# Attention tower with a routed feed-forward part: heads multiplied on GpSimd, evictions moved to ScalarE, two gate buffers, and the last batch's quarters interleaved

## The chip, the cores and the metric

The kernel runs on one core of one Trainium2 chip. The metric is the device time of one execution in microseconds (us). The engines are TensorE (PE in the rows; its weight loads are PEld), VectorE (DVE), ScalarE (ACT), GpSimd (POOL) and SyncE (SP), which here only issues DMAs.

## The reference

```python
h = tok(x)                       # gather per token: sin/cos waves @ W_proj + biases, (8, 1024, 512)
h = h + attn(layernorm(h))       # 16 heads of 32; S = K Q^T * scale, causal, minus (i - j);
                                 # softmax over j, times V, then @ o_w.T
h = h + ffn(layernorm(h))        # scores = sqrt(softplus(h @ gate_w.T)); top 6 of 32 experts;
                                 # place of a token in an expert = count of earlier choices, at most 192;
                                 # silu(g) * u per expert; plus a shared expert: clip(silu(sg h) * (su h), 10) @ sd.T
```

All of it is float32, for 8 batches of 1024 tokens.

## The kernel before

The program has three parts, run one after the other: `embed` (the gathers, the first layernorm, which writes `d_hidden` and the transposed `d_normed_t` to HBM), `attend` (attention, router and shared expert, which scatters each token's normalised row to its six places in `d_slots`), and `experts` (the 32 routed experts, added to `out`). The change is in `attend`.

`attend` first projects q, k and v of two head groups (12 projections, the prologue), while SyncE loads constants. Then it walks over 32 steps: 8 batches of 4 head groups (g = 0 to 3, four heads each). A step has 12 slots, m = 0 to 11. Slots 0 to 3 are the score tiles of the first 512 query rows, slots 4 to 11 those of the second 512. In each slot TensorE does the scores of the slot (`scores`, L1309, with the shift L1313 and the mask L1319), the product with the values of the slot before (`attend_group`, L1332), and row scores for the next step's maxima (`row_scores`, L1285). ScalarE turns the scores into probabilities (`soften`, L872), GpSimd adds them up (`add_probs`, L806) into `first_probs`, two buffers `probs` going round, and VectorE takes row maxima (`row_maxima`, L994).

In between, at three gaps A, B and C of each slot, lie the uses of one PSUM bank, `ps_dense`, in an order fixed at build time (`plan`): the projections for a later step (`project`, L1273 and L1269), the sums of the probabilities (`sum_probs`, L1341), the turned row maxima (`turn_maxima`, L1292), the output projection of the batch before (`out_project`, L1352, only in g = 0), and one quarter (256 tokens) of the router and shared expert of the batch before: `turn` (L1360), `route` (L1367), `up` twice (L1375), `place` (`count_earlier`, L1391), `down` twice (L1383). Each use waits until the one before has been taken out of the bank (`dense_free`). In before, VectorE takes out the values (L986) and the row shifts (L1008), ScalarE the projections of q and k, the sums (L885), the turned rows and the gate inputs (L903, L904).

VectorE's division of the heads by the sums (`divide_heads`) is cut into four pieces of 128 columns for each half of a step: a reciprocal (L1015) and a multiply (L1018) each, in slots 1 to 4 (late half of the step before) and 6, 8, 9, 10 (early half). `out_project` and the next `take_sums` wait for `heads_done`, given by the fourth piece. VectorE's queue in slot 10 is: row maxima, the early half's fourth piece, `gate(x, 1)` (L1153 plus one, L1155 reciprocal, L1158 and L1160 multiplies, L1162 clamp), then `find_places`, whose first instruction (L1127) empties the bank. TensorE's next use is `down` at slot 11, gap A.

After the 32 steps the last batch still lacks its output projections and its four quarters. Before, these run one after the other: eight `out_project` with `add_residual` and a store and reload through `d_hidden`, then four times `quarter` (statistics, normalise, turn, route, up, choose, place, down), each ending in 12 scatters by GpSimd (L810). `experts` begins when all is stored.

## Time and profile before

| | |
|---|---|
| time of the kernel, median of 3 runs | 3867.13 us (3866.15 to 3868.62) |
| profiled execution: its own time, its span | 3872.97 us, 3871.2 us |
| mean granted TensorE clock | 0.920 of full |
| busy over the span: PE, DVE, ACT, POOL | 84%, 63%, 29%, 43% |
| last `embed` DMA issue, first projection of `attend` | 249.32 us, 281.15 us |
| first step begins, first tail quarter's `down` | 367 us, 766 us |
| the 32 steps end, the `experts` loads begin | about 3323 us, 3541.29 us |

Times in the profile are microseconds from the start of the span. A busy share is an average over the whole span; what a part of the change is worth has to be read from its own stretch.

### The profile page before, as it was taken

The page shows a single profiled execution, that of the slowest core. Times are in us where ns is not written, and L with a number is a line of the kernel's source. Part 1 is how long each engine was busy: PE and PEld are TensorE (multiplying, and loading weights), DVE is VectorE, ACT ScalarE, POOL GpSimd, SP SyncE. Part 2 cuts the span into 40 slices and gives each one's busy share as a digit, 9 for nine tenths or more (in the row PEclk, how much of TensorE's full clock was granted, in tenths as well). Part 3 has the DMA queues.
Part 4 walks back from the last instruction along what each step waited for, and adds up shares of the span by engine and source line. Part 5 has one row for each costly group of instructions (what it writes and reads, how often), then busy time and mean ns, then how long its engine had stood idle before and what let it go on. Part 6 is the DMA issues. An engine that isn't in the chain of part 4 may idle for free. (4 is left out here: it accounts for less than half of the span.)

```text
span 3871.2 us, 62509 instructions
## 1 busy us (share of the span) xinstructions
PE 3245.3 (84%) x20296; PEld 1670.1 (43%) x20296; DVE 2419.5 (63%) x6622; ACT 1112.7 (29%) x2553; POOL 1671.2 (43%) x924
## 2 busy tenths in 40 slices
PE   4647999888888888888888888889888977655998
PEld 2324444444444444444444444444444433334776
DVE  6733565567667665766576657665776577553554
ACT  3751333233223322332233223322332233101111
POOL 5630354445435443544454445444444446322332
PEclk8878999999999999999999999999999988867999
DMA  5664000021111011101010101010101000104996
GB/s 199 244 271 136 1 28 20 28 77 50 68 51 46 14 34 34 34 12 39 29 34 12 40 28 34 12 40 28 34 12 39 28 12 12 55 25 133 259 259 154
DMA packets 123205, 257.87 MB, mean 67 GB/s; under 512 B 38988, under 2 KB 39628, under 8 KB 120192
## 3 DMA queue, kind: packets, MB, share of 16 engines
q1 hardware_dynamic: 78400, 201.42, 15.8%
q0 software_dynamic: 44048, 49.26, 5.0%
q8 instruction: 169, 2.77, 0.3%
q10 hardware_dynamic: 432, 3.15, 0.2%
q14 instruction: 156, 1.28, 0.1%
HBM read 146.71 MB, written 204.26 MB: 91 GB/s over the span
## 5 line engine op out<-in xcount | busy, mean ns | idle before, releaser
L806 POOL TENSOR_TENSOR a_first_probs<-a_first_probs,a_probs 128x2048 f32<-128x2048 f32 (+3 forms) x320 | 1033.5, 3230 | 1594.1 <-ACT a_probs L872 1375.0
L994 DVE CUSTOM_DVE_ANT_0 a_unused<-a_ps_ring,a_decay 128x512 bf16<-128x512 f32 (+3 forms) x1536 | 773.4, 554 | 515.8 <-PE a_ps_ring L1285 510.2
L872 ACT ACTIVATE a_probs<-a_ps_ring 128x512 f32<-128x512 f32 (+3 forms) x1280 | 505.5, 473 | 794.8 <-PE a_ps_ring L1319 600.1
L810 POOL DMA_INDIRECT d_slots<-a_rows,a_place_i x397 | 395.6, 997 | 226.3 <-DVE a_place_i L1147 141.7
L1309 PE MATMUL a_ps_ring<-a_k_t,a_q_t 32*128 32x512 f32 (+3 forms) x3072 | 412.6, 539 | 72.4 <-DVE a_row_max L994 44.0
L1285 PE MATMUL a_ps_ring<-a_q_t,a_k_t 32*128 32x512 f32 (+3 forms) x3072 | 391.3, 542 | 17.5 <-DVE a_row_max L994 12.6
L1383 PE MATMUL a_ps_dense<-a_sd,a_inner_t 128*128 128x512 f32 x256 | 184.5, 860 | 191.3 <-DVE a_gate_up L1127 188.0
L1273 PE MATMUL a_ps_dense<-a_normed_t,a_q_w 128*128 128x512 f32 x512 | 246.0, 625 | 35.1 <-DVE a_max_cols L980 32.5
L872 ACT ACTIVATE a_first_probs<-a_ps_ring 128x512 f32<-128x512 f32 x256 | 135.6, 605 | 475.8 <-PE a_ps_ring L1319 450.9
L1332 PE MATMUL a_ps_heads<-a_probs,a_values 128*32 128x512 f32 (+3 forms) x2560 | 269.9, 495 | 0.0
L1309 PEld LDWEIGHTS a_ps_ring<-a_k_t,a_q_t 32*128 32x128 f32 x3072 | 146.0, 186 | 274.9 <-issue 147.0
L1352 PE MATMUL a_ps_dense<-a_o_w,a_attn_t 128*128 128x512 f32 x512 | 237.9, 608 | 18.3 <-DVE a_values L986 10.5
L1273 PE MATMUL a_ps_dense<-a_normed_t,a_k_w 128*128 128x512 f32 x512 | 238.4, 609 | 15.7 <-DVE a_residual L1025 9.7
L1269 PEld LDWEIGHTS a_ps_dense<-a_v_w,a_normed_t 128*128 128x128 f32 x2048 | 235.1, 193 | 36.5 <-issue 35.5
L1269 PE MATMUL a_ps_dense<-a_v_w,a_normed_t 128*128 128x128 f32 x2048 | 247.3, 279 | 1.7 <-ACT a_k_t L857 0.9
L1015 DVE RECIPROCAL a_sum_inv<-a_sum_inv 128x128 f32<-128x128 f32 x256 | 242.6, 948 | 1.9 <-ACT a_sum_inv L885 1.9
L1285 PEld LDWEIGHTS a_ps_ring<-a_q_t,a_k_t 32*128 32x128 f32 x3072 | 144.8, 187 | 225.2 <-issue 189.6
L1018 DVE TENSOR_TENSOR a_attn_t<-a_attn_t,a_sum_inv 128x128 f32<-128x128 f32 x256 | 221.8, 866 | 14.3 <-DVE a_sum_inv L1015 0.9
L1008 DVE CAST a_row_shift<-a_ps_dense 128x512 bf16<-128x512 f32 x64 | 44.3, 692 | 238.0 <-PE a_ps_dense L1292 238.0
L1651 POOL DMA_INDIRECT out<-x_y,x_index x64 | 90.2, 1409 | 236.1 <-DMA out<-x_y,x_index 151.9
L1383 PEld LDWEIGHTS a_ps_dense<-a_sd,a_inner_t 128*128 128x128 f32 x256 | 59.8, 259 | 272.7 <-DVE a_inner_t L1162 158.3
L1273 PEld LDWEIGHTS a_ps_dense<-a_normed_t,a_q_w 128*128 128x128 f32 x512 | 95.7, 197 | 160.2 <-issue 152.8
(177 smaller groups left out, 4402.2 us busy)
## 6 DMA issues: line engine op xcount, KB each, us to landing
d_hidden<-e_hidden SPq DMA_DIRECT2D x8, 2048.0 KB, 7.9
d_normed_t<-e_normed_t SPq DMA_DIRECT2D x8, 2048.0 KB, 11.6
a_normed_t<-d_normed_t SPq DMA_DIRECT2D x8, 2048.0 KB
a_residual<-d_hidden SPq DMA_DIRECT2D x64, 256.0 KB
d_hidden<-a_residual SPq DMA_DIRECT2D x64, 256.0 KB
a_hidden<-d_hidden SPq DMA_DIRECT2D x64, 256.0 KB
out<-a_hidden SPq DMA_DIRECT2D x64, 256.0 KB
x_w_gate<-w_gate SPq DMA_DIRECT2D x32, 512.0 KB, 6.3
```

The lines of the kernel that those rows point to most:

```text
L806: nc.gpsimd.tensor_tensor(total_of, total_of, probs_of(m)[:, :, 0:width], ALU.add).then_inc(added, 1)
L810: nc.gpsimd.indirect_dma_start(slot_rows, bass.IndirectOffsetOnAxis(ap=place_i[p][:, j, choice:choice + 1], axis=0), rows[p][:, j, :], Non ...
L872: nc.scalar.activation(probs_of(m)[:, h, 0:width], score_bank(m, h)[:, 0:width], ACT.Exp).then_inc(exp_done, 1)
L994: nc.vector.tensor_tensor_reduce(unused[:, h, 0:width], row_bank(k, h)[:, 0:width], decay[:, at:at + width], 1.0, NEG, ALU.add, ALU.max, r ...
L1015: nc.vector.reciprocal(sum_inv[half][:, cols], sum_inv[half][:, cols]).then_inc(sums_inverted, 1)
L1269: mm = nc.tensor.matmul(ps_dense[:, t * P:(t + 1) * P], normed_t[:, c, tile * P:(tile + 1) * P], w[:, c, g * P:(g + 1) * P], start=(c == 0 ...
L1273: mm = nc.tensor.matmul(ps_dense[:], w[:, c, g * P:(g + 1) * P], normed_t[:, c, half_cols(half)], start=(c == 0), stop=(c == DC - 1))
L1285: nc.tensor.matmul(row_bank(k, h)[:, 0:width], k_t[g][dims, i * P:(i + 1) * P], q_t[g][dims, j0:j0 + width], start=True, stop=True).then_i ...
L1309: nc.tensor.matmul(score_bank(m, h)[:, 0:width], q_t[st.g][dims, j * P:(j + 1) * P], k_t[st.g][dims, i0:i0 + width], start=True, stop=False)
L1332: mm = nc.tensor.matmul(ps_heads[dims, at], values[g][:, j, dims], probs_of(m)[:, h, 0:width], start=(j == 0), stop=(j == last_j))
L1352: mm = nc.tensor.matmul(ps_dense[:], attn_t[:, g, i * P:(i + 1) * P], o_w[:, g, :], start=(g == 0), stop=(g == G - 1))
L1383: mm = nc.tensor.matmul(ps_dense[:], inner_t[:, m, j * P:(j + 1) * P], sd[:, m, :], start=(m == 0), stop=(m == MC - 1))
```

## The change

- `divide_heads` is split. VectorE keeps the four reciprocals (`invert_sums`); GpSimd multiplies a whole half, 128x512, at once (`multiply_heads`), before its add of slot 5 (late half) and slot 11 (early half), and gives `heads_done`.
- ScalarE takes the values and the row shifts out of `ps_dense`.
- The gate: `exp` goes into `inner_t`, ScalarE adds the one there, and each of the two `up` halves has its own `gate_up` buffer; VectorE's gate has four instructions for five. The wait of ScalarE for `inner_done` in `soften_gate` is gone.
- Router: two small instructions are folded into others, `counts` (float32) is dropped for running counts in bf16, updated in `find_places`; `count_earlier` has four small matmuls for two.
- The scratch output `unused` has three parts instead of four. GpSimd gives `rows_free` in slot 0 instead of slot 1.
- After the 32 steps: all eight residual tiles are loaded to SBUF at once into q and k tiles that are no longer in use (not stored and reloaded), PSUM uses go round four banks of the score ring, and output projections, statistics, normalising and turning of quarter q + 1 are placed between the parts of quarter q (`late_uses`). Each quarter has its own row buffer and places.
- First loads: the first half of `normed_t` is loaded by itself, the biases of q and k go to ScalarE's queue behind `q_w`; TensorE waits for the constants only before `turn_maxima`; the 33 stores that empty the slots are issued after the prologue.

The tables of slots (`QUARTER_AT`, `STATS_AT`, ...) hold the same slots as before.

```diff
+            def multiply_heads(s, g, half):
+                heads = attn_t[:, g, half_cols(half)]
+                pool.wait_ge(heads_taken, 2 * s + half + 1)
+                pool.wait_ge(sums_inverted, PIECES * (2 * s + half + 1))
+                nc.gpsimd.tensor_tensor(heads, heads, sum_inv[half][:], ALU.mult).then_inc(heads_done, 1)
...
             def step(st):                                    # GpSimd
                 for m in range(N_GROUPS):
+                    if m == LATE_MULTIPLY and not st.first:
+                        multiply_heads(st.s - 1, (st.g - 1) % G, 1)
+                    if m == EARLY_MULTIPLY:
+                        multiply_heads(st.s, st.g, 0)
                     add_probs(st, m)
...
+            def take_values(g, half, use):                   # ScalarE; VectorE's is gone
+                act.wait_ge(use.full, use.n + 1)
+                nc.scalar.activation(values[g][:, half_tiles(half), :], use.bank[:].rearrange("p (t m) -> p t m", m=P),
+                                     ACT.Identity).then_inc(use.free, 1)
...
+            def take_maxima(p, half, use):                   # ScalarE; VectorE's is gone
+                act.wait_ge(use.full, use.n + 1)
+                nc.scalar.activation(row_shift[p][:, half_cols(half)], use.bank[:], ACT.Identity).then_inc(use.free, 1)
...
-                if m > 0:
-                    act.wait_ge(inner_done, MC * x + m)
-                act.wait_ge(dense_full, n + 1)
-                nc.scalar.activation(gate_e[:], ps_dense[:, 0:2 * P], ACT.Exp, scale=-1.0).then_inc(gate_e_done, 1)
-                nc.scalar.activation(gate_up[:], ps_dense[:], ACT.Identity).then_inc(dense_free, 1)
+                act.wait_ge(use.full, use.n + 1)
+                nc.scalar.activation(inner_t[:, m, :], use.bank[:, 0:2 * P], ACT.Exp, scale=-1.0).then_inc(gate_e_made, 1)
+                nc.scalar.activation(gate_up[m][:], use.bank[:], ACT.Identity).then_inc(use.free, 1)
+                act.wait_ge(gate_e_made, MC * x + m + 1)
+                nc.scalar.activation(inner_t[:, m, :], inner_t[:, m, :], ACT.Identity, bias=1.0).then_inc(gate_e_done, 1)
...
-            def divide_heads(s, g, half, piece, n):          # VectorE
+            def invert_sums(half, piece, use):
+                cols = slice(piece * HALF // PIECES, (piece + 1) * HALF // PIECES)
+                dve.wait_ge(use.free, use.n + 1)
                 nc.vector.reciprocal(sum_inv[half][:, cols], sum_inv[half][:, cols]).then_inc(sums_inverted, 1)
-                dve.wait_ge(heads_taken, 2 * s + half + 1)
-                dve.wait_ge(sums_inverted, PIECES * (2 * s + half) + piece + 1)
-                instruction = nc.vector.tensor_tensor(heads, heads, sum_inv[half][:, cols], ALU.mult)
...
                 if st.g == G - 1:                            # SyncE
-                    for i in range(2):
-                        load_residual(st.b, i)
+                    if st.rows:
+                        for i in range(2):
+                            load_residual(st.b, i)
+                    else:
+                        sp.wait_ge(scores_full, ITEMS * (FINAL - 2))
+                        for i in range(NT):
+                            sp.dma_start(late_hidden[i], dram["hidden"][NB - 1, tile_rows(i), :]).then_inc(late_in, 16)
...
+    uses = out(0, 0) + out(0, 1) + [("sums", 1, None)] + turn(0, 0) + turn(0, 1)
+    for q in range(QUARTERS):
+        uses += [("route", 0, q), ("up", 0, q)] + out(q + 1, 0) + [("up", 1, q)] + out(q + 1, 1) + [("place", 0, q)]
+        uses += turn(q + 1, 0) + turn(q + 1, 1) + [("down", 0, q), ("down", 1, q)]
...
+            def quarter(q):                                  # VectorE, last batch
+                soft_parts(late("route", 0, q), chain)
+                soft_sum(x, chain)
+                gate(x, 0, late("up", 0, q), chain)
+                if more:
+                    add_late(2 * q + 2, late("out", 2 * q + 2))
+                choose(x, chain)
+                if more:
+                    add_late(2 * q + 3, late("out", 2 * q + 3))
+                    take_late_stats(q + 1, norm)
+                count_chosen(chain)
+                if more:
+                    normalise_late(q + 1, norm)
+                gate(x, 1, late("up", 1, q), chain)
+                find_places(x, q, late("place", 0, q), chain)
+                for j in range(2):
+                    add_shared(late_hidden[2 * q + j], late("down", j, q))
...
-            pe.wait_ge(consts_in, 16 * N_CONSTS)             # TensorE
-            pe.wait_ge(consts_made, N_MADE)
...
-            pe.wait_ge(normed_in, 16)
+            pe.wait_ge(normed_half_in, 16)
             for n, (kind, half) in enumerate(PROJECTIONS * 2):
+                if n == 2:
+                    pe.wait_ge(normed_in, 16)
...
+            sp.wait_ge(dense_full, N_PROLOGUE)               # SyncE, before the 33 stores
```

## Rows read from the trace of the kernel before

**Rows 1.** Busy time by stretch (last steps and after): us, each engine, granted clock, DMA share, GB/s

```profile
770.00:3130.00 2360.00, 2099.12 (x14101) 1013.78 (x14094) 1579.80 (x4558) 705.27 (x1686) 1092.57 (x543) 0.95 0.11 34
3130.00:3325.00 195.00, 141.42 (x986) 64.91 (x986) 145.93 (x340) 56.73 (x144) 105.57 (x55) 0.82 0.05 14
3325.00:3545.00 220.00, 116.20 (x328) 69.46 (x328) 91.61 (x276) 18.81 (x50) 56.93 (x58) 0.73 0.14 42
```

**Rows 2.** Waits of TensorE, 770 to 3130: total us, times, longest

```profile
PE a_ps_dense L1383 <- DVE a_gate_up L1127: 153.9, 24, 6.7
PE a_ps_dense L1375 <- DVE a_values L986: 29.0, 19, 1.5
PE a_ps_ring L1309 <- DVE a_row_max L994: 17.7, 37, 0.8
...
PE a_ps_dense L1352 <- DVE a_values L986: 9.0, 6, 1.6
```

**Rows 3.** Timeline, 1026 to 1032, one quarter's end: start, us, instruction

```profile
1026.09 1.49 DVE L1018 TENSOR_TENSOR a_attn_t<-a_attn_t,a_sum_inv 128x128 f32<-128x128 f32 x1
1026.13 1.29 POOL L806 TENSOR_TENSOR a_first_probs<-a_first_probs,a_probs 128x512 f32<-128x512 f32 x1
...
1027.51 0.28 DVE L1153 TENSOR_SCALAR a_gate_e<-a_gate_e 128x256 f32<-128x256 f32 x1
...
1030.83 0.55 DVE L1127 TENSOR_TENSOR a_gate_up<-a_is_top,a_ps_dense 128x384 f32<-128x384 bf16 x1
...
1031.51 3.78 PE L1383 MATMUL a_ps_dense<-a_sd,a_inner_t 128*128 128x512 f32 x4 [6.34 <-DVE a_gate_up L1127]
```

**Rows 4.** The multiplies L1018, 770 to 3130: shortest/median/longest ns

```profile
L1018 DVE TENSOR_TENSOR a_attn_t<-a_attn_t,a_sum_inv x197: 291/805/2187, 787.0 to 3117.7; 128x128 f32<-128x128 f32 x197
```

**Rows 5.** Busy time by stretch, two microseconds inside that `down`

```profile
1034.00:1036.00 2.00, 2.00 (x10) 0.20 (x8) 0.68 (x1) 0.00 (x0) 0.00 (x0) 0.50 0.00 0
```

**Rows 6.** Groups of GpSimd by form, 900 to 3100

```profile
L806 POOL TENSOR_TENSOR a_first_probs<-a_first_probs,a_probs 128x512 f32<-128x512 f32 x46 | 58.6, 1274 | 81.7 <-ACT a_probs L872 81.5
```

**Rows 7.** Groups of VectorE by form, 900 to 3100: count | busy, mean ns | idle before

```profile
L986 DVE COPY a_values<-a_ps_dense 128x512 f32<-128x512 f32 x46 | 31.5, 686 | 0.8 <-issue 0.8
```

**Rows 8.** Groups of ScalarE by form, 900 to 3100

```profile
L904 ACT ACTIVATE a_gate_up<-a_ps_dense 128x512 f32<-128x512 f32 x46 | 27.2, 592 | 0.0
```

**Rows 9.** Waits of TensorE, 3130 to 3325, the last batch's steps

```profile
PE a_ps_dense L1383 <- DVE a_gate_up L1127: 14.4, 3, 6.2
PE a_ps_ring L1309 <- ACT a_probs L872: 14.0, 6, 5.7
PE a_ps_ring L1309 <- DVE a_row_max L994: 10.9, 8, 5.1
PE a_ps_dense L1391 <- DVE a_counts L1116: 7.8, 2, 4.6
```

**Rows 10.** Timeline after the 32 steps, 3325 to 3542

```profile
3325.55 3.70 PE L1352 MATMUL a_ps_dense<-a_o_w,a_attn_t 128*128 128x512 f32 x8 [0.78 <-ACT a_sum_inv L885]
...
3372.95 0.23 DVE L1058 TENSOR_SCALAR a_plus<-a_ps_dense 128x64 f32<-128x64 f32 x1 [6.92 <-PE a_ps_dense L1367]
...
3394.87 0.98 POOL L810 DMA_INDIRECT d_slots<-a_rows,a_place_i  x1 [57.34 <-DVE a_place_i L1147]
...
3535.26 0.98 POOL L810 DMA_INDIRECT d_slots<-a_rows,a_place_i  x1 [0.30 <-issue]
...
3541.29 0.34 SPq L1505 DMA_DIRECT2D x_ident<-c_ident  x1
```

**Rows 11.** Timeline of the first loads and the first projection

```profile
259.79 0.43 ACTq L845 DMA_DIRECT2D a_q_w<-q_w  x1
...
281.15 5.87 PE L1273 MATMUL a_ps_dense<-a_normed_t,a_q_w 128*128 128x512 f32 x8 [32.48 <-DVE a_max_cols L980]
```

**Rows 12.** DMA issues, 225 to 345: KB each, median us to landing

```profile
a_q_w<-q_w ACTq DMA_DIRECT2D x1, 1024.0 KB, 9.5
```

**Rows 13.** Timeline of the first batch, a projection behind slot 11's row maxima

```profile
444.31 6.22 PE L1273 MATMUL a_ps_dense<-a_normed_t,a_q_w 128*128 128x512 f32 x8
```

More of the change, by code:

```diff
@@ L450 @@
 N_PROBS = 2
+N_UNUSED = HG - 1
 ADDS = N_GROUPS - 2
@@ L453 @@
 SOFT_LEAST = 2.0 ** -62
-PIECES = HALF // P
 QUARTERS = 4
@@ L651, in attend, with late, dense @@
         N_CONSTS = len(consts) + 3
-        N_MADE = 3
+        N_MADE = 2
         FREE = 16
         SCATTERS = 16 * 2 * TOPK
-        TAIL_STEPS = 49
+        NORM_STEPS, TAIL_STEPS = 8, 35
+        @dataclass
+        class Use:
+            bank: object
+            full: object
+            free: object
+            n: object
+        def late(kind, arg, q=None):
+            n = next(n for n, (k, a, u) in enumerate(LATE) if (k, a) == (kind, arg) and (q is None or u == q))
+            k = n % LATE_BANKS
+            return Use(ps_ring[k], late_full[k], late_free[k], n // LATE_BANKS)
+        def dense(n):
+            return Use(ps_dense, dense_full, dense_free, n)
         def shape(m):
@@ L1028, in take_stats, with take_late_stats @@
+            def take_late_stats(q, norm):
+                for j in range(2):
+                    use = late("out", 2 * q + j)
+                    dve.wait_ge(use.free, use.n + 1)
+                take_stats(late_hidden[2 * q:2 * q + 2], norm)
+            def take_stats(tiles, chain):
                 dve.wait_ge(tail_consts_in, 16 * len(tail_consts))
                 for j in range(2):
-                    dve.wait_ge(hidden_in[j], 16 * (x + 1))
-                    chain.done(nc.vector.bn_stats(stats[:, j, :], hidden[j][:]))
+                    chain.done(nc.vector.bn_stats(stats[:, j, :], tiles[j]))
@@ L1177, in take_dense, with add_shared @@
+            def add_shared(tile, use):
+                dve.wait_ge(use.full, use.n + 1)
+                nc.vector.tensor_tensor(tile, use.bank[:], tile, ALU.add).then_inc(use.free, 1)
+            def take_dense(st, slot, gap, chain):
+                for kind, arg, k in st.uses[slot][gap]:
+                    use = dense(st.base + k)
+                    if kind == "out":
+                        add_residual(st.t, arg, use)
                     elif kind == "route":
-                        soft_parts(n, chains[0])
+                        soft_parts(use, chain)
@@ new lines, in tail_events @@
+            def tail_events(st, m, after, norm, chain):
+                x, first = QUARTERS * st.t + st.g, st.g == 0
+                if (m, after) == STATS_AT[first]:
+                    for j in range(2):
+                        dve.wait_ge(hidden_in[j], 16 * (x + 1))
+                    take_stats([tile[:] for tile in hidden], norm)
+                if (m, after) == NORMALISE_AT[first]:
+                    dve.wait_ge(rows_free, x + 1)
+                    normalise(x, rows[st.g % 2], [tile[:] for tile in hidden], norm)
+                if (m, after) == SOFT_SUM_AT[first]:
@@ L1252, in _ @@
+            norm = norm_chain(0)
+            take_late_stats(0, norm)
+            for piece in range(PIECES):
+                invert_sums(1, piece, late("sums", 1))
+            normalise_late(0, norm)
             for q in range(QUARTERS):
```

536 lines of the change are left out of this document (272 added, 264 removed).

## The prediction, made before the changed kernel was run

> **What bounds the kernel now.** I read the busy time by stretch first [rows 1]. Over 770 to 3130 (24 steps with a tail quarter) TensorE is busy 2099 of 2360 us, 89%; nothing else is above 67%. So TensorE sets the pace, and a change can win only the 261 us in which it stands still there, and time lost to its clock. In the last batch's steps TensorE is busy 73%, VectorE 75%; after the steps, 53% at a granted clock of 0.73.
>
> Next, the waits of TensorE in the first of these stretches [rows 2]. One wait is more than half of all idle time: `down` behind L1127, 153.9 us in 24 times, 6.4 us each, once per quarter. Then 38.0 us behind VectorE's eviction of values (L1375 and L1352), and 17.7 us behind row maxima.
>
> The timeline says what makes that one wait [rows 3]. `down` waits for the bank, the bank for L1127, and L1127 for its place in VectorE's queue: the last piece of the division, then the gate. The multiply L1018 of 128 columns takes 1.49 us there, and ends 0.16 us after GpSimd's add L806, which runs at the same time. Over the steady part L1018 takes 805 ns at the median against 291 ns at its shortest [rows 4]: it stretches when a GpSimd add runs. After the stall the granted clock is 0.50, that is 1.2 GHz instead of 2.4 [rows 5], and the four matmuls of `down` take 3.78 us, about twice what the second `down` of the same quarter takes.
>
> **The change part by part.**
>
> *The division.* VectorE loses 8 multiplies per step, 8 x 0.8 = 6.4 us of its queue [rows 4]. GpSimd gains two 128x512 operations, 2 x 1.27 = 2.5 us [rows 6]. In the slot-10 queue the multiply's 1.49 us goes, and L1153's 0.28 us with it [rows 3], since ScalarE adds the one in good time. The row maxima of slot 10 start earlier too: values are not evicted before them (0.69 us [rows 7]). Together 1.49 + 0.28 + 0.7 = 2.5 us less per quarter. Against it stands one new collision. GpSimd's multiply waits for the fourth reciprocal, so it runs right beside the gate's reciprocal, and its add of slot 11 follows at once, with no DMA issue between. The gate's two multiplies read two SBUF tiles, as L1018 does, and would wait for whichever runs. Bounds: 0.1 us (VectorE gets in as the multiply ends) to 1.3 us (it sits through the add as well). I take 0.6 us, nearer to the first, because L1018 in [rows 3] starts within 0.2 us of the add's end. So 1.9 us per quarter (1.2 to 2.4) over the 25 such quarters before 3130: 47 us (30 to 60).
>
> The rule for this in the Trainium skill, "SBUF — State Buffer", section "Who interferes with whom", is that a VectorE instruction with two SBUF inputs and a GpSimd one that reads SBUF exclude each other for the whole instruction. The trace agrees: L1018 takes 1.49 us there against 0.29. By the rule applied without mercy the gate would sit through multiply and add, and the gain per quarter would be 1.2 us. "GPSIMD Engine Reference", section "4.1 Engine selection", speaks against the move itself: elementwise work belongs on VectorE, GpSimd is about twice as slow with two inputs. This trace doesn't bear that out at this size: 1.27 us on GpSimd against 4 x 0.29 = 1.16 on VectorE undisturbed.
>
> *Evictions on ScalarE.* The values: ScalarE has nothing before it in its queue but exps long due, so the 38.0 us of [rows 2] go; all of them, because TensorE has scores to do between that projection and its next use of the bank. The row shifts cut the other way. In slots 1 and 5 ScalarE still has two exps to do when the turned maxima are ready, where VectorE had been waiting for them; a copy of 592 ns [rows 8] after them ends some 0.15 us later than the row scores that hide it. Twice in 32 steps: 0.3 x 32 = 10 us lost (0 to 20).
>
> *Gate buffers, router.* The second buffer removes a ScalarE wait that ends before `up` is ready anyhow: 0. Fewer small VectorE instructions shorten slots 8 and 9, where TensorE doesn't wait in the steady part: 0, covered by the v projection in slot 9. The two added matmuls of `place`: about 0.2 us x 28 = 6 us lost. `unused` in three parts: the first maximum is long done when the fourth starts, 0. `rows_free` earlier: GpSimd is idle there, 0.
>
> *Row maxima.* VectorE catches up sooner; of the 17.7 us I take 8. In the first batch one wait of this kind per step is followed by a stretch at 0.50 clock in which a projection takes 6.22 us [rows 13] instead of 3.70; I take 5 us of waits and 7 of clock (half of 4 steps x 3.4).
>
> *GpSimd late half.* Its multiply in slot 5 comes before an add of 4.5 us. Before that add GpSimd is idle some 11 us in the timeline, but the fourth reciprocal comes only about 2 us before the add starts; 1.27 us fits. Behind it in the queue stand this add and the scatters; who waits for the add is ScalarE, two slots on. 0, and if the reciprocal came 1 us later, 0.3 us of it would be seen. `heads_done` comes 1 to 2 us later, ten microseconds ahead of `out_project`.
>
> *Last batch's steps.* 54 us of waits; the four of [rows 9] make 47. From `down` 3 x 1.9 = 6, from `place` (late VectorE) 5, from row maxima 5, from exps (ScalarE behind a VectorE that GpSimd holds up) 4: 20 us (8 to 32; GpSimd is the tightest in the last step, where slots take 6 us and an add with a scatter 5.9).
>
> *After the steps.* Before: 3325.5 to 3541.3, 215.8 us [rows 10]: eight projections, then four quarters, the later ones (3535.3 - 11 x 1.28 - 3394.9)/3 = 42 us apart. New: two projections end at about 3331; but `add_late` waits for all eight loads, which SyncE issues behind the last `store_out`, from about 3324 on, with 2 MB to bring: 3335.5. Statistics 1.7, four reciprocals 3.8 (they stand between statistics and normalising), normalise 1.7, turns 3.5, route 3.6: `soft_parts` at 3351 instead of 3373. A quarter then cannot be shorter than TensorE's work, 116.2/4 = 29 us [rows 1], nor longer than before with its projections, 50.6. Following the queues (up 3.9, projection 3.7, up, projection, statistics and normalise, gate, `down` twice, route of the next, partly at the lower clock) I get 33 us. Three of them, then the last quarter's 21.9 us from L1058 to the first scatter, 12 scatters in 15.4 us, and 6.0 us from the last one to `experts` [rows 10]: 3351 + 99 + 22 + 15 + 6 = 3493, 48 us saved (21 to 60, the ends being 42 us and 29 us a quarter).
>
> *First loads.* TensorE starts when `q_w` and half of `normed_t` are in. `q_w` is issued at 259.79 and lands 9.5 us later, at 269.3 [rows 11, 12], against a start at 281.15 behind the constants. k and v weights land at 272.5 and 275, before they are used; the constants still come before the first maxima. 11 us (7 to 12). The stores into the slots run later under the first steps; who needs them is GpSimd's scatter in the second batch, 350 us on: 0.
>
> The sum against the profiled execution, 3872.97: 47 + 38 + 8 + 12 + 20 + 48 + 11 = 184 won, 16 lost, 168 in all: 3705. The median of the runs lies 5.8 us below the profiled one: 3699. Of the steady stall's clock loss (5.3 us at half speed after each stall, 2.65 us x 28 = 74 us) I count only a tenth, since shorter waits than 4.4 us are followed by the lower clock in this trace too: 7. **3692 us.**
>
> **The rivals.**
>
> *The collision takes the place of the multiply* (0.2). The gate is held through GpSimd's multiply and add, and each of its later instructions meets the next GpSimd one. For it: L1018 itself, stretched from 0.29 to 0.8 at the median. Against: L1158 and L1160 never stretched before in the steady part. Then nothing of the 47 + 6 us is left: 3745.
>
> *The clock holds* (0.15). With 4.4 us for 6.4 TensorE comes back while still at 2.4 GHz, or soon returns to it. For: the step is very regular, so what happens once happens 24 times. Against: in the first batch 2.4 us of waits are enough for the lower clock. Then most of the 74 us comes on top: 3692 - 60 = 3632.
>
> *The late pipeline doesn't pipeline* (0.07). All eight loads and VectorE's single queue hold each quarter at the old 42 us: 21 us saved instead of 48: 3719.
>
> *GpSimd becomes the bound; slower than before* (0.04). Its multiply in slot 5 waits at the head of its queue for VectorE's fourth reciprocal; the 4.5 us adds slip, `probs` buffers come free late, exps and scores with them. It decides from 5.3 us per step on (168/32), against the 2 us of slack and GpSimd's 46% share [rows 1]. At 6 us per step: 3889.
>
> **How the numbers follow.** The forecast has 0.54, its own range 3655 to 3725: the ends of its terms, not all at once. With the collision and the late pipeline above it and most of the clock case below, the range for 8 in 10 is 3625 to 3750. A measurement of this kernel tells about 0.2%, 8 us, from no change. Faster 0.95, within 0.01, slower 0.04.
>
> **What would show it.** Right: the wait of `down` behind L1127 near 4.4 us, none behind values, L1153 and L1018 gone, first projection at 270, the `experts` loads some 170 us after the last `attend_group` instead of 218. Wrong: `down` still at 6 us with L1158 stretched beyond 0.43 us; waits behind ScalarE's evictions of row shifts above 0.3 us; a mean granted clock clearly above 0.95 between the steps; GpSimd's slot-5 multiply starting after the exps of slot 5.

## The result, and the profile after

The changed kernel takes **3718.6 us** (median of 4 runs, 3716.9 to 3725.4) against 3867.9 us of the kernel before on the same chip (4 runs, 3866.2 to 3872.9): ratio 0.9615, 95% interval 0.9599 to 0.9632. 149 us are gone; 3692 us were forecast, in a range of 3625 to 3750. The profiled execution took 3716.85 us (span 3715.1, granted clock 0.935 instead of 0.920), against 3872.97: 156.1 us less.

Where they went is read from five marks in both timelines: the start of the first `down` (L1383 before, L1472 after), of the `down` 24 quarters later (the last batch's first), of the last one in the steps, the first load of `experts`, and the end of the span.

| stretch, us | before | after | gained |
|---|---|---|---|
| start to the first `down` | 765.9 | 742.7 | 23.2 |
| 24 quarters | 2297.0 (95.7 each) | 2230.3 (92.9 each) | 66.6 |
| last batch's steps, first to last `down` | 253.5 | 242.9 | 10.7 |
| last `down` to `experts`' first load | 224.9 | 169.9 | 55.0 |
| `experts` | 329.9 | 329.3 | 0.6 |

Busy time by stretch, after (us, then PE, PEld, DVE, ACT, POOL, granted clock, DMA share, GB/s), the three stretches that answer to [rows 1]:

```profile
745.00:3040.00 2295.00, 2096.25 (x14159) 1018.90 (x14158) 1387.64 (x4123) 773.35 (x1834) 1157.51 (x592) 0.96 0.11 35
3040.00:3222.00 182.00, 136.02 (x967) 62.36 (x966) 134.03 (x294) 59.81 (x151) 112.07 (x59) 0.82 0.05 14
3222.00:3390.00 168.00, 101.24 (x356) 63.44 (x355) 84.78 (x251) 21.95 (x59) 58.54 (x59) 0.76 0.11 32
```

The first of them and that of [rows 1] hold nearly as many quarters each, 24.7. TensorE is as busy as before; its idle time fell from 261 to 199 us. TensorE's waits in the same stretch (total us, times, longest), which answer to [rows 2]:

```profile
PE a_ps_dense L1472 <- DVE a_gate_up L1203: 128.3, 24, 5.4
PE a_ps_ring L1398 <- DVE a_row_max L1084: 24.6, 37, 0.7
PE a_ps_dense L1449 <- ACT a_rows_t L976: 19.2, 25, 0.8
```

No wait behind values is left. The wait of `down` fell from 6.4 to 5.35 us, not to 4.4. The timeline of one quarter's end shows why; beside [rows 3], L1018 and L1153 are gone, and L1234 (L1158 before) has become long:

```profile
995.02 0.95 DVE L1099 RECIPROCAL a_sum_inv<-a_sum_inv 128x128 f32<-128x128 f32 x1
...
995.88 1.70 DVE L1231 RECIPROCAL a_inner_t<-a_inner_t 128x256 f32<-128x256 f32 x1
996.05 1.28 POOL L862 TENSOR_TENSOR a_attn_t<-a_attn_t,a_sum_inv 128x512 f32<-128x512 f32 x1
997.27 1.27 POOL L855 TENSOR_TENSOR a_first_probs<-a_first_probs,a_probs 128x512 f32<-128x512 f32 x1
997.70 1.13 DVE L1234 TENSOR_TENSOR a_inner_t<-a_gate_up,a_inner_t 128x256 f32<-128x256 f32 x1
...
999.33 0.49 DVE L1238 TENSOR_SCALAR a_inner_t<-a_inner_t 128x256 f32<-128x256 f32 x1
999.75 0.54 DVE L1203 TENSOR_TENSOR a_gate_up<-a_is_top,a_ps_dense 128x384 f32<-128x384 bf16 x1
...
1000.41 3.40 PE L1472 MATMUL a_ps_dense<-a_sd,a_inner_t 128*128 128x512 f32 x4 [5.35 <-DVE a_gate_up L1203]
```

The gate's first multiply, 0.43 us when nothing is in its way, starts at 997.70 inside GpSimd's addition (997.27 to 998.54) and ends at 998.83, just behind it. That is 0.70 us of the 1.73 us that L1018 and L1153 gave back (before, from L1018's start at 1026.09 to L1155's at 1027.82). The clamp L1238 takes 0.49 us instead of 0.29; beside it GpSimd issues a scatter (998.71 to 999.72).

The first projection and the stretch behind the steps, in the timeline, which answer to [rows 10, 11]:

```profile
271.81 5.90 PE L1362 MATMUL a_ps_dense<-a_normed_t,a_q_w 128*128 128x512 f32 x8 [22.21 <-DMA a_normed_t<-d_normed_t]
...
3223.55 7.13 PE L1441 MATMUL a_ps_ring<-a_o_w,a_attn_t 128*128 128x512 f32 x16
...
3248.01 0.23 DVE L1146 TENSOR_SCALAR a_plus<-a_ps_ring 128x64 f32<-128x64 f32 x1 [5.93 <-PE a_ps_ring L1456]
...
3276.89 1.00 POOL L866 DMA_INDIRECT d_slots<-a_rows,a_place_i  x1 [36.07 <-DVE a_place_i L1225]
...
3365.56 0.98 POOL L866 DMA_INDIRECT d_slots<-a_normed_t,a_place_i  x1 [9.40 <-DVE a_place_i L1225]
...
3385.77 0.34 SPq L1604 DMA_DIRECT2D x_ident<-c_ident  x1
```

From the first out projection to `soft_parts` 24.5 us instead of 47.4, and from the first quarter's first scatter to the last quarter's (88.7 us apart) 29.6 us per quarter instead of 42.

### The profile page after: what moved, and what is told of

It is laid out like the page before. It is cut to its first block and busy times, and to the rows that moved or that the text cites. A ratio compares the mean times of both kernels' runs of the same rounds, so it can differ in the third digit from the quotient of the medians.

```text
span 3715.1 us, 61950 instructions
## 1 busy us (share of the span) xinstructions
PE 3207.5 (86%) x20352; PEld 1660.1 (45%) x20360; DVE 2157.7 (58%) x6046; ACT 1201.6 (32%) x2745; POOL 1756.5 (47%) x988
## 3 DMA queue, kind: packets, MB, share of 16 engines
q14 instruction: 148, 1.21, 0.1%
## 5 line engine op out<-in xcount | busy, mean ns | idle before, releaser
L1398 PE MATMUL a_ps_ring<-a_k_t,a_q_t 32*128 32x512 f32 (+3 forms) x3072 | 412.0, 538 | 66.6 <-DVE a_row_max L1084 44.4
L866 POOL DMA_INDIRECT d_slots<-a_rows,a_place_i x373 | 379.2, 1017 | 134.4 <-issue 71.6
L1472 PE MATMUL a_ps_dense<-a_sd,a_inner_t 128*128 128x512 f32 x224 | 158.8, 848 | 147.4 <-DVE a_gate_up L1203 147.4
L1362 PE MATMUL a_ps_dense<-a_normed_t,a_q_w 128*128 128x512 f32 x512 | 240.5, 613 | 24.7 <-DMA a_normed_t<-d_normed_t 22.2
L862 POOL TENSOR_TENSOR a_attn_t<-a_attn_t,a_sum_inv 128x512 f32<-128x512 f32 x64 | 81.6, 1274 | 280.3 <-DVE a_sum_inv L1099 279.7
L1441 PE MATMUL a_ps_dense<-a_o_w,a_attn_t 128*128 128x512 f32 x448 | 206.2, 603 | 1.1 <-ACT a_row_shift L965 0.2
L1362 PEld LDWEIGHTS a_ps_dense<-a_normed_t,a_k_w 128*128 128x128 f32 x512 | 92.3, 190 | 143.4 <-issue 112.4
L1402 PE MATMUL a_ps_ring<-a_row_shift,a_key_shift 5*128 5x512 bf16 (+3 forms) x1536 | 154.7, 328 | 0.0
```

Of the source, the lines that this page charges most:

```text
L866: nc.gpsimd.indirect_dma_start(slot_rows, bass.IndirectOffsetOnAxis(ap=place_i[p][:, j, choice:choice + 1], axis=0), late_rows[p][:, j, :] ...
L1362: mm = nc.tensor.matmul(use.bank[:], w[:, c, g * P:(g + 1) * P], normed_t[:, c, half_cols(half)], start=(c == 0), stop=(c == DC - 1))
L1398: nc.tensor.matmul(score_bank(m, h)[:, 0:width], q_t[st.g][dims, j * P:(j + 1) * P], k_t[st.g][dims, i0:i0 + width], start=True, stop=False)
L1441: mm = nc.tensor.matmul(use.bank[:], attn_t[:, g, i * P:(i + 1) * P], o_w[:, g, :], start=(g == 0), stop=(g == G - 1))
```

## The experiments

All start from the changed kernel. Each was timed in 5 rounds beside the kernel before, whose median was 3869 to 3872 us; 8 us decide. One more thing varies between the profiles in the first stretch: up to the first `down`, `late_serial` has the instructions of the changed kernel, yet it gets there at 749.8 us instead of 742.7, with a granted clock of 0.97 instead of 1.00 from 380 to 500 us (the kernel before has 0.97 there). Some 7 us of a profile can be this; what decides between the two is not shown.

### The division back on VectorE: `divide_back`

```diff
-                nc.gpsimd.tensor_tensor(heads, heads, sum_inv[half][:], ALU.mult).then_inc(heads_done, 1)
...
+                dve.wait_ge(sums_inverted, PIECES * (2 * s + half) + piece + 1)
+                instruction = nc.vector.tensor_tensor(heads, heads, sum_inv[half][:, cols], ALU.mult)
```

> The changed kernel (3718.6 us) with the division wholly on VectorE again, four multiplies of 128x128 a half, and no multiply on GpSimd. Theory 1 (the multiply on GpSimd shortens VectorE's chain ahead of the down matmuls, but only by what is left after a collision): the stall ahead of L1472 goes from 5.35 us to 6.1 to 6.5, about as before the change, and the kernel loses 28 quarters by 0.8 to 1.1 us, 22 to 31 us, plus up to 12 us for the four late pieces: 3740 to 3762. Rival (the multiply gained nothing there; the 1.0 us that the stall lost came from the one that adds 1 and from the clock): 3718 within 8 us, stall 5.2 to 5.6.

Measured: 3754.6 us (ratio 0.9698, 0.9683 to 0.9714), 36 us slower. Theory 1 holds. The waits of `down`:

```profile
PE a_ps_dense L1466 <- DVE a_gate_up L1197: 154.4, 25, 6.3
```

This is nearly as much as before the change, 6.2 us each for 6.4. In the 24 quarters the division is worth 25 us (2255.4 against 2230.3), a little over 1 us each.

### Is the gate held by GpSimd? `invert_slot7` and `multiply_slot10`

```diff
-LATE_INVERT, EARLY_INVERT = (1, 2, 3, 4), (6, 8, 9, 10)
+LATE_INVERT, EARLY_INVERT = (1, 2, 3, 4), (6, 7, 8, 9)
...
-LATE_MULTIPLY, EARLY_MULTIPLY = 5, 11
+LATE_MULTIPLY, EARLY_MULTIPLY = 5, 10
```

The first has the first pair of lines alone, the second both.

> The early reciprocals stand in slots 6, 7, 8, 9 instead of 6, 8, 9, 10, so the 0.95 us reciprocal of slot 10 leaves the chain row maxima, reciprocal, gate, down. GpSimd's multiply stays in slot 11, before its addition. Theory 1 (the gate's first multiply is held until GpSimd's addition of slot 11 ends, at 998.54 us in the profiled quarter): the reciprocal of the gate ends 0.95 us sooner, its multiply starts 0.95 us sooner and is held 0.95 us longer, about 2.1 us in all instead of 1.13; the stall stays at 5.2 to 5.4 us and the time within 8 us of 3718.6. Rival (VectorE's own instructions alone set the stall): stall 4.4 us, 28 quarters by 0.95 us = 27 us faster, 3692.

Measured: 3716.6 us (0.9606, 0.9587 to 0.9626), stall 5.3 us in every quarter (128.1 us, 24 times). Taking 0.95 us out of VectorE's queue ahead of the gate gains nothing: the rival falls. The timeline of the same place shows where it went. The gate's first multiply now takes 1.93 us:

```profile
995.59 1.93 DVE L1234 TENSOR_TENSOR a_inner_t<-a_gate_up,a_inner_t 128x256 f32<-128x256 f32 x1
995.95 1.28 POOL L855 TENSOR_TENSOR a_first_probs<-a_first_probs,a_probs 128x512 f32<-128x512 f32 x1
```

In all 24 quarters of 745 to 3040 it takes 1.93 to 2.04 us, where the changed kernel has 1.13 to 1.27. GpSimd, not VectorE's own work, set the gate's end.

> The same early reciprocals in slots 6 to 9, and GpSimd's early multiply in slot 10 ahead of that slot's addition instead of in slot 11. Theory 1 (collision): GpSimd's addition of slot 11 now runs about 1.2 us sooner, the gate's multiply waits 0.5 us at most, and the stall falls to 3.8 to 4.2 us: 28 quarters by 1.2 to 1.5 us, 33 to 42 us faster than the changed kernel, 3677 to 3686, of which the multiply now in slot 9 to 10 may give back up to 8 us by holding the count of chosen experts. Rival (no collision): the same as with the reciprocals moved alone, 3692.

Measured: 3724.8 us (0.9619, 0.9604 to 0.9634), no gain. The stall did fall, to 4.1 us at most (94.9 us in 24 times), as Theory 1 had it, but both theories had the time wrong. What was gained came back elsewhere. TensorE's waits, and the place in the timeline where they come from:

```profile
PE a_ps_dense L1472 <- DVE a_gate_up L1203: 94.9, 24, 4.1
PE a_ps_dense L1480 <- DVE a_chosen_b L1196: 40.1, 18, 2.8
```

```profile
991.64 3.66 DVE L1196 CAST a_chosen_b<-a_soft_ln 128x64 bf16<-128x64 f32 x1
991.64 1.31 POOL L862 TENSOR_TENSOR a_attn_t<-a_attn_t,a_sum_inv 128x512 f32<-128x512 f32 x1
...
992.87 2.36 POOL L855 TENSOR_TENSOR a_first_probs<-a_first_probs,a_probs 128x1024 f32<-128x1024 f32 x1
```

A cast of 128x64 that takes 0.20 us in the changed kernel takes 3.66, through GpSimd's multiply and the addition behind it. I had foreseen this at 8 us at most; it cost 40 us of waits. The multiply had been moved from one thing that matters to another.

### The second gate earlier: `gate_slot9` and `gate9_invert7`

```diff
-GATE_AT = {True: ((7, 1), (10, 1)), False: ((7, 1), (10, 1))}
+GATE_AT = {True: ((7, 1), (9, 1)), False: ((7, 1), (9, 1))}
```

The second has the early reciprocals in slots 6 to 9 as well.

> The second gate (reciprocal 1.70 us, two multiplies, clamp) is computed at the end of slot 9, after the count, instead of at the end of slot 10. VectorE stands idle for 1.5 us there in the profiled quarter, so the row maxima of slot 10 start about 2.2 us later than now and end about 2.2 us later, and behind them only the reciprocal 0.95 and the multiply L1203 0.54 stand before the bank is free. Theory 1: down starts 1.0 to 1.5 us sooner, 28 to 42 us faster: 3677 to 3691, while TensorE's wait for the row maxima at slot 11's scores grows by up to 2.2 us and the stall at the down matmuls shrinks to about 2 us. Rival (the later row maxima cost as much as the gate gains): 3718 within 8 us.

Measured: 3697.5 us (0.9548, 0.9533 to 0.9563), 21 us faster, short of the 28 to 42. The stall is nearly gone, but it has moved:

```profile
PE a_ps_ring L1398 <- DVE a_row_max L1084: 97.3, 38, 3.8
PE a_ps_dense L1472 <- DVE a_gate_up L1203: 24.2, 24, 1.4
```

121.5 us of waits instead of 152.9. In its timeline the gate's first multiply takes 1.77 us through the addition of slot 10, which my 1.0 to 1.5 us for the whole part had not allowed for.

> The second gate in slot 9 (alone: 3697.5 us, 21 us faster than the changed kernel) and the early reciprocals in slots 6 to 9 (alone: 3716.6, no change). Theory 1 (VectorE's queue from the count to L1203 bounds slot 10; the reciprocal moved out was worth nothing only because GpSimd's addition held the gate, and with the gate gone ahead nothing holds it): the 0.95 us reciprocal leaves the path, down starts up to 0.9 us sooner: 15 to 25 us faster than 3697.5, 3672 to 3683. Rival (the parts add up): 3695.5 within 8 us.

Measured: 3705.9 us (0.9571, 0.9556 to 0.9585): not faster than `gate_slot9`, 8 us slower, at the edge of what can be told. Neither theory had it. The `down` wait is gone (1.3 us in all), and the row maxima's has grown to 117.0 us: with the reciprocals done early GpSimd multiplies at once, and now the clamp is held, an instruction with a single input:

```profile
991.11 1.83 DVE L1238 TENSOR_SCALAR a_inner_t<-a_inner_t 128x256 f32<-128x256 f32 x1
991.50 1.29 POOL L862 TENSOR_TENSOR a_attn_t<-a_attn_t,a_sum_inv 128x512 f32<-128x512 f32 x1
```

### The evictions: `values_back`, `divide_values_back`, `maxima_back`

```diff
-                nc.scalar.activation(values[g][:, half_tiles(half), :], use.bank[:].rearrange("p (t m) -> p t m", m=P),
-                                     ACT.Identity).then_inc(use.free, 1)
+                nc.vector.tensor_copy(values[g][:, half_tiles(half), :],
+                                      use.bank[:].rearrange("p (t m) -> p t m", m=P)).then_inc(use.free, 1)
```

> The changed kernel (3718.6 us) with the values evicted by VectorE again (0.69 us each, 64 of them), everything else as changed. Theory 1 (on VectorE these evictions stand behind the row maxima and hold the single dense bank): the waits behind the values come back, 38 us of them before the change; 3745 to 3757. Rival (those waits had only stood where another wait for VectorE would have stood, so moving them gained a part): 3728 to 3740.

Measured: 3722.6 us (0.9618, 0.9601 to 0.9635), 4 us and no difference that counts. Both theories fall: the waits behind values come back as 5.7 us in 6 times, not 38.

> The changed kernel with both the division and the evictions of values on VectorE again; each alone measured 36 us and 4 us slower than the changed kernel's 3718.6. Theory 1 (the 38 us of waits behind the values came from VectorE running late behind the division, so that either edit alone removes them): they come back only now: 3754.6 + 25 to 38 = 3780 to 3793, with 20 to 38 us of TensorE's waits behind values. Rival (the two parts add up): 3754.6 + 4 = 3759, within 8 us.

Measured: 3758.6 us (0.9713, 0.9700 to 0.9727). The parts add up; the waits behind values are 5.7 us again. So neither the eviction nor the division had made the 38 us. The timelines of slot 7 show what is left; first the kernel before:

```profile
1001.36 4.53 POOL L806 TENSOR_TENSOR a_first_probs<-a_first_probs,a_probs 128x2048 f32<-128x2048 f32 x1 [1.54 <-ACT a_probs L872]
...
1003.80 2.24 DVE L1153 TENSOR_SCALAR a_gate_e<-a_gate_e 128x256 f32<-128x256 f32 x1
...
1009.08 0.68 DVE L986 COPY a_values<-a_ps_dense 128x512 f32<-128x512 f32 x1
...
1009.82 1.99 PE L1375 MATMUL a_ps_dense<-a_rows_t,a_sg 128*128 128x256 f32 x8 [1.54 <-DVE a_values L986]
```

and `divide_values_back`:

```profile
982.38 4.53 POOL L855 TENSOR_TENSOR a_first_probs<-a_first_probs,a_probs 128x2048 f32<-128x2048 f32 x1 [1.54 <-ACT a_probs L929]
...
984.82 1.75 DVE L1221 RECIPROCAL a_inner_t<-a_inner_t 128x256 f32<-128x256 f32 x1
986.69 0.50 DVE L1224 TENSOR_TENSOR a_inner_t<-a_gate_up,a_inner_t 128x256 f32<-128x256 f32 x1
...
988.10 0.67 DVE L1058 COPY a_values<-a_ps_dense 128x512 f32<-128x512 f32 x1
...
989.23 1.99 PE L1459 MATMUL a_ps_dense<-a_rows_t,a_sg 128*128 128x256 f32 x8
```

In slot 7 of the kernel before, the instruction that adds 1, 0.29 us by itself, started inside GpSimd's 4.53 us addition and took 2.24 us. The gate behind it, the eviction behind the gate and TensorE's wait of 1.54 us all follow. With the addition of 1 on ScalarE the gate begins with a reciprocal, which takes its usual 1.75 us beside GpSimd, and its multiply comes as GpSimd ends and takes 0.50 us. Counted from the start of GpSimd's addition, the eviction comes at 5.72 us instead of 7.72.

The whole steady part of the kernel before agrees. From 770 to 3130 TensorE waits behind the values 19 times at L1375, and each of these waits ends 6.0 us after the start of an L1153 that took 2.23 to 2.25 us; in the quarters of g = 0, where L1153 of slot 7 took 0.29 us, L1375 has no such wait. The list of groups, 900 to 3100, had a sign of it, a mean of 1006 ns for an instruction of 0.28:

```profile
L1153 DVE TENSOR_SCALAR a_gate_e<-a_gate_e 128x256 f32<-128x256 f32 x46 | 46.3, 1006 | 0.0
```

The additions of 1 were not put back alone, so this cause is read from timelines and not tested. The six waits at L1352, 9.0 us, are another case: they are there in `values_back` too, with 5.7 us, and these the eviction on ScalarE does remove.

The row shifts go back by the same edit in `take_maxima`.

> The changed kernel with the row shifts evicted by VectorE again (64 evictions, 0.3 to 0.7 us each). Theory 1 (this part neither gained nor lost, since the evictions of row shifts were waited for on neither engine): 3718.6 within 8 us. Rival A (on ScalarE they stand behind exps, so taking them back gains up to 10 us): 3708 to 3713. Rival B (VectorE's time in slots 1 and 5 was short, so taking them back loses 28 x 2 x 0.3 us): 3735.

Measured: 3726.7 us (0.9626, 0.9608 to 0.9644), 8 us slower, at the edge of what can be told. Of the three cases Rival A falls: the move to ScalarE cost nothing. Between Theory 1 and Rival B this does not decide.

### The last batch one quarter after the other: `late_serial`

```diff
-        uses += [("route", 0, q), ("up", 0, q)] + out(q + 1, 0) + [("up", 1, q)] + out(q + 1, 1) + [("place", 0, q)]
-        uses += turn(q + 1, 0) + turn(q + 1, 1) + [("down", 0, q), ("down", 1, q)]
+        uses += [("route", 0, q), ("up", 0, q), ("up", 1, q), ("place", 0, q), ("down", 0, q), ("down", 1, q)]
+        uses += out(q + 1, 0) + out(q + 1, 1) + turn(q + 1, 0) + turn(q + 1, 1)
```

VectorE's `quarter` is ordered to match.

> The changed kernel with the last batch's quarters one after the other: both out projections, statistics, normalisation and turn of quarter q+1 follow the down projection of quarter q on TensorE and VectorE; four banks, early loads and late tiles stay. Theory 1 (the pipeline hides most of the next quarter's front): three fronts of add 1.4, statistics 1.4, rstd 2, normalisation 1.5, turn and eviction 2.5 and route, about 10 to 14 us each, come back on the path: 30 to 42 us slower, 3749 to 3761. Rival (what shortened the stretch was loading the residuals early and no longer storing and loading each tile, not the order): 3722 to 3733.

Measured: 3749.1 us (0.9685, 0.9666 to 0.9704), 30 us slower, Theory 1. The last `down` of the steps starts at 3223.21, the first load of `experts` at 3419.16: 196.0 us, between the 169.9 of the changed kernel and the 224.9 of before. The order is worth 26 us of the 55; the other 29 are left for the early loads, the four banks and the stores left out, none of which was put back alone.

### TensorE waits for the constants again: `first_wait_back`

```diff
+            pe.wait_ge(consts_made, N_MADE)
             pe.wait_ge(normed_half_in, 16)
```

> The changed kernel with TensorE waiting for the constants (all five loads and the copies made of them) before its first projection, as before the change; the loads' new order stays. Theory 1 (that wait alone held the first projection at 281 us instead of 272): first projection at 279 to 282 us, 7 to 10 us slower, 3726 to 3729. Rival (the row maxima of the first step need the same constants, so that the projections' head start is lost at once): 3718.6 within 3 us.

Measured: 3734.5 us (0.9647, 0.9631 to 0.9663), 16 us slower. The first projection starts at 281.92:

```profile
281.92 5.71 PE L1362 MATMUL a_ps_dense<-a_normed_t,a_q_w 128*128 128x512 f32 x8 [32.85 <-DVE a_max_cols L1074]
```

That is 10.1 us later, and the same 8.6 us remain at the first scores. The rival falls. The rest up to 16 us stays open; in this profile the granted clock from 380 to 500 us is 0.97, as in `late_serial`.

### Versions that keep the gate out of GpSimd's way: `split_gate` and `gate_first`

```diff
                     count_chosen(chain)
+                    invert_gate(x, 1, chain)
                 if (m, after) == GATE_AT[first][1]:
-                    gate(x, 1, dense(st.number("up", 1)), chain)
+                    gate(x, 1, dense(st.number("up", 1)), chain, inverted=True)
```

`invert_gate` is the gate's reciprocal; the reciprocals of the sums stand in slots 6 to 9.

> Early reciprocals in slots 6 to 9, and of the second gate only the reciprocal (1.70 us) in slot 9, in the 1.5 us in which VectorE stood idle; its two multiplies and the clamp stay in slot 10 behind the row maxima, where GpSimd's addition of slot 10 is over and that of slot 11 hasn't begun. Theory 1 (VectorE's queue and the collisions set the stall): behind the row maxima of slot 10 only 0.43 + 0.43 + 0.49 + 0.54 = 1.9 us stand before the bank is free instead of 5.2, so the stall of down falls from 5.35 us to 1.8 to 2.6 us and the wait behind the row maxima stays under 1 us: 28 quarters by 2.7 to 3.5 us = 76 to 98 us, less some collision: 3625 to 3650. Rival (the gate's first multiply meets GpSimd's multiply of slot 11 and its addition and is held for 1 to 2.5 us): stall 3 to 4.5 us, 3665 to 3690. Neither counts a gain of clock; if the shorter stall also spares TensorE its lower clock, up to 2 us a quarter come on top.

Measured: 3703.8 us (0.9568, 0.9552 to 0.9584), 15 us faster: outside both ranges, but with the rival's mechanism, at a higher price than its 1 to 2.5 us:

```profile
1001.10 3.31 DVE L1241 TENSOR_TENSOR a_inner_t<-a_gate_up,a_inner_t 128x256 f32<-128x256 f32 x1
1001.61 1.29 POOL L862 TENSOR_TENSOR a_attn_t<-a_attn_t,a_sum_inv 128x512 f32<-128x512 f32 x1
1002.83 1.29 POOL L855 TENSOR_TENSOR a_first_probs<-a_first_probs,a_probs 128x512 f32<-128x512 f32 x1
```

One multiply of 0.43 us takes 3.31, through two instructions of GpSimd, and the stall is 4.67. `gate_first` takes away what holds it, and puts `attend_group` ahead of `down`:

```diff
-QUARTER_AT = {True: ((4, A), (4, B), (5, C), (6, C), (8, C), (10, C), (11, A), (11, C)),
+QUARTER_AT = {True: ((4, A), (4, B), (5, C), (6, C), (8, C), (10, C), (11, B), (11, C)),
...
+                    if m == N_GROUPS - 1 and st.t is not None:
+                        pool.wait_ge(inner_done, MC * (QUARTERS * st.t + st.g + 1))
                     add_probs(st, m)
...
+                    if m == EARLY_MULTIPLY:
+                        multiply_heads(st.s, st.g, 0)
```

The last two lines stand behind the slot's scatter.

> A version meant to keep the gate out of GpSimd's way: as split_gate (early reciprocals in slots 6 to 9, the second gate's reciprocal in slot 9, its rest in slot 10), and GpSimd waits for the gate before its addition of slot 11, and multiplies only behind that addition and the slot's scatter; the first down stands behind attend_group of slot 10. Theory 1 (in split_gate the gate's second multiply was held 3.31 us through GpSimd's multiply and addition, and this alone kept its stall at 4.67 us): the second multiply takes at most 0.9 us (it may still end with the scatter of slot 10), down's wait is 1.5 to 2.4 us, 0.6 us of it because attend_group now stands ahead of it; 28 quarters by 2.9 to 3.8 us = 81 to 106 us faster than the changed kernel in waits, 3612 to 3638, if nothing waits for the later addition. Rival (the later addition and multiply hold the count, the places or the exps instead): 3650 to 3690, with new waits behind L1480, L1398 or the exps of more than 30 us.

Measured: **3628.7 us** (5 runs, 3624.7 to 3633.1; ratio 0.9371, 0.9350 to 0.9391), 90 us faster than the changed kernel and 241 us faster than the one before. Theory 1 holds. TensorE's waits over 745 to 3040, and one quarter's end:

```profile
PE a_ps_dense L1482 <- DVE a_gate_up L1207: 30.3, 25, 1.2
PE a_ps_ring L1408 <- DVE a_row_max L1088: 28.4, 42, 1.3
PE a_ps_dense L1482 <- DVE a_hidden L1251: 22.7, 24, 2.1
```

```profile
985.42 0.42 DVE L1245 TENSOR_TENSOR a_inner_t<-a_gate_up,a_inner_t 128x256 f32<-128x256 f32 x1
985.88 0.29 DVE L1247 TENSOR_SCALAR a_inner_t<-a_inner_t 128x256 f32<-128x256 f32 x1
...
986.42 1.26 POOL L855 TENSOR_TENSOR a_first_probs<-a_first_probs,a_probs 128x512 f32<-128x512 f32 x1 [0.49 <-DVE a_inner_t L1247]
...
986.77 3.48 PE L1482 MATMUL a_ps_dense<-a_sd,a_inner_t 128*128 128x512 f32 x4 [1.21 <-DVE a_gate_up L1207]
...
988.83 1.30 POOL L862 TENSOR_TENSOR a_attn_t<-a_attn_t,a_sum_inv 128x512 f32<-128x512 f32 x1
```

128 us of waits have become 53 (30.3 and 22.7; the second `down` now waits for the addition to `hidden`, which stands behind the places). The 24 quarters take 2154.8 us instead of 2230.3, 89.8 each. Beside `split_gate` this version changes two things at once, GpSimd's order and `attend_group` ahead of `down`. The gate's multiplies of 0.45 and 0.42 us show what the first does; `attend_group` fills 0.64 us of the former stall at the place shown. What each is worth in time was not measured.

## Why the prediction was right, and where it was not

The bound was named rightly: TensorE's idle time, most of it at `down`. The sum was 27 us too good, and two of its terms, the values and the first batch, were near in size without their reasons having been right or shown.

- **The down stall.** The term of 1.9 us a quarter was mis-sized: 1.0 us, 26 us over 24 quarters instead of 46. The 1.49 and 0.28 us went as worked out, and the collision was 0.7 us against the 0.6 taken. That this was so near is partly luck: the reason given for 0.6 was misread, since in [rows 3] L1018 starts at 1026.09, beside the add's start, and it is its end that comes within 0.2 us of the add's. The step that failed is "the row maxima of slot 10 start earlier too", 0.7 us: they wait for the row scores (VectorE stands idle 1.50 us ahead of them, at 993.09), so the eviction ahead of them had cost nothing. The kernel before shows the same: its row scores end at 1023.03 and its row maxima start at 1023.20, 0.17 us later with the eviction just ahead of them, and in the changed kernel it is 0.17 us as well (992.92 and 993.09). The rest is the clamp's 0.2. `divide_back` puts the whole part at 36 us. The rival in which the collision takes everything falls with it, but `invert_slot7` shows that the collision had become the bound: a further 0.95 us saved ahead of the gate was lost in it. The sentence beside the term, by the Trainium skill's "SBUF — State Buffer", section "Who interferes with whom", came to 1.2 us a quarter and so nearer to the measured 1.0 than my 1.9.
- **GpSimd's speed.** The prediction has one 128x512 multiply on GpSimd, 1.27 us, level with four of 128x128 on VectorE, 1.16 us. That sets one instruction against four. The same trace has VectorE's multiply of the same size, two inputs in SBUF, at 0.68 us (L266, in `embed`): GpSimd is 1.9 times as slow, and so the trace does bear out the factor of two that the prediction set aside.
- **The values.** The 38 us of waits went, as forecast, and the step that explains them failed. "ScalarE has nothing before it in its queue but exps long due, so the 38.0 us of [rows 2] go" took the waiting instruction's releaser for the cause. `values_back` and `divide_values_back` leave 5.7 us of these waits with VectorE evicting. By the timelines the cause of the 29.0 us at L1375 was L1153 in slot 7, held 2.24 us, for which the prediction had no term: it priced L1153 in slot 10 alone, at 0.28. [Rows 2] named who released; the timeline of that slot, or L1153's mean of 1006 ns, would have named who was late.
- **Row maxima.** Wrong in sign, by a little: 24.6 us instead of 17.7, where 8 less were taken; and the waits behind `rows_t` (L1449) are now 19.2 us.
- **Row shifts on ScalarE.** The loss of 10 us isn't there: the waits for them are 0.4 us over 745 to 3040, and `maxima_back` is not faster. The lower bound, 0, was right.
- **The clock.** Busy time fell by 0.25 us a quarter, 6 us over 24, against 7 taken. The case in which the clock holds did not come: `down` runs at 3.4 to 3.8 us behind each stall of 5.3.
- **The first loads and the first batch.** 11 + 12 us against 23.2 measured, 9.3 up to the first projection and 13.9 behind it. That the sum fits so well is luck: some 7 us of a profile can lie in the clock of this stretch, and waits and clock of the first batch were not taken apart. The wait for the constants is the whole of the earlier start, as `first_wait_back` shows.
- **The last batch's steps.** 20 us were taken (8 to 32), some 9 measured: 7.8 from the second `down` to the fourth, and 1.5 from there to the first out projection. The term for `place` failed: TensorE waits 9.5 us there once, and 13.2 in all, where [rows 9] had 7.8. In the timeline VectorE comes late because GpSimd's additions hold it: in the last step four of its instructions, each at most 0.3 us at its shortest, take 4.92, 5.04, 4.67 and 3.25 us beside them (L1155, L1160, L1238, L1172). The kernel before has three above 3 us, 4.82, 4.80 and 4.49 us (L1018, L1072, L1162). One of the four, and the wait:

```profile
3187.77 5.04 DVE L1160 TENSOR_TENSOR a_soft<-a_soft,a_soft_w 128x64 f32<-128x64 f32 x1
3188.15 4.56 POOL L855 TENSOR_TENSOR a_first_probs<-a_first_probs,a_probs 128x2048 f32<-128x2048 f32 x1
...
3210.52 0.21 PE L1480 MATMUL a_ps_dense<-a_chosen_b,a_before_b 128*128 128x64 bf16 x1 [9.55 <-DVE a_chosen_b L1196]
```

- **After the steps.** 216 us down to 168 were forecast, by the first out projection and `experts`' first load; 162.2 measured (3385.8 - 3223.6). To `soft_parts` 24.5 us against 25.5 forecast; a quarter 29.6 against 33. `late_serial` shows the order to be worth 26 us.
- **GpSimd as the bound, slower** did not come: of TensorE's waits over 745 to 3040 only 7.3 us are behind exps, 4.4 and 2.9, none of them above 0.5 us. The time given for this case was wrong by its own terms: 6 us in each of 32 steps on top of 3692 is 3884, not 3889.

The parts put back one by one come to 36 + 4 + 8 + 30 + 16 = 94 us of the 149; the 4 and the 8 can't be told from nothing. What is left lies with what was never put back alone: the addition of 1 and its buffers (by the timelines most of the 2297.0 - 2252.2 = 44.8 us by which the 24 quarters of `divide_values_back` are shorter than those of the kernel before), and the loads and banks of the last batch (29 us). Why `first_wait_back` loses 16 us and not 10 stays open.

## What to carry to other kernels

A wait's releaser is the last instruction of a queue, not its cause: go back along that queue until one instruction takes longer than it does elsewhere. A group whose mean is far above its shortest instruction is the place to start. Where VectorE and GpSimd share a stretch, when their instructions run is worth more than how many they are: moving 1.5 us of work from VectorE to GpSimd gained 1.0 us a quarter, and reordering, with no work removed, so that the gate's arithmetic meets none of GpSimd's, gained another 3.1 (92.9 to 89.8, with `attend_group` ahead of `down` included). Before an instruction is moved out of the way of one, look at what it then stands beside.

## What the runs showed of the hardware

GpSimd's arithmetic held VectorE in more than instructions with two SBUF inputs: a cast of 128x64 took 3.66 us instead of 0.20, a clamp with one input 1.83 instead of 0.29, the addition of 1 2.24 instead of 0.29. Reciprocals (1.70 to 1.75 us for 128x256) and the row maxima (0.55 us for 128x384), which read PSUM and SBUF, kept their time beside the same GpSimd instructions. The Trainium skill, "SBUF — State Buffer", section "Who interferes with whom", lists copies, casts and `tensor_scalar` among those that can take the shared pair of ports when their operands meet its conditions; these rows agree.

Nor did VectorE get in between two GpSimd instructions that follow each other at once: the 3.66 and 3.31 us last through multiply and addition both. Beside a scatter the gate's second multiply ran undisturbed (0.43 us at 998.87 in the changed kernel, scatter from 998.71 to 999.72), while the clamp behind it took 0.49 us instead of 0.29.

The clock fell behind each wait of 5.3 us that I looked at, and not behind each of 1.2: in `gate_first` the first `down`, after 1.23 us, ran in 1.98 us at a granted clock of 1.00 (2.4 GHz), the one at 986.77, after 1.21 us, in 3.48 at 0.50 (1.2 GHz). Its clock from 740 to 2894 us was 0.98 against 0.96 in the changed kernel.
